# Attention scores in quarters of the array, with both sequences in one stacking transfer

## What is computed

```python
x = x + _L0_xattn_ref(_layernorm(x), ctx_1024, ctx_1024, ...)
#   scores = einsum('bhqd,bhkd->bhqk', q, k) / sqrt(8); softmax; @ v; @ Wo.T + bo
x = x + _L0_ffn_ref(_layernorm(x), ...)
#   out_branch: top 32 of softmax(gate_out) times (x @ weight)
#   in_branch:  (x times top 32 of softmax(gate_in)) @ weight
```

## Time and profile before

| | us |
|---|---|
| median of 3 runs (558.95 to 564.75) | 564.16 |
| the profiled execution | 563.33 |
| its span, first to last instruction | 560.8 |
| attention stage, to the first top-k work | about 311 |
| top-k stage and its end | about 250 |

### The profile page before, as it was taken

How to read it: one execution, slowest core, us unless ns; L and a number is a source line. 1 busy time by engine, 2 the same in 40 slices (tenths; PEclk the granted TensorE clock), 3 DMA queues, 4 the chain that set the end, 5 groups by cost and what they waited for, 6 DMA issues and landing times.

```text
span 560.8 us, 15570 instructions
## 1 busy us (share of the span) xinstructions
PE 405.9 (72%) x5186; PEld 316.1 (56%) x5186; DVE 440.5 (79%) x2165; ACT 375.1 (67%) x1060; POOL 330.2 (59%) x402
## 2 busy tenths in 40 slices
PE   3467988999998999988992766666666666666432
PEld 1135766777777777777860545545555555445331
DVE  7745666777877777776541799999999999999990
ACT  2425676877788777766655967777677666676652
POOL 6466676887677777562112046666666666666666
PEclk9857999999999999999795555555555555555555
DMA  4888786888887887675000000000000000000000
GB/s 135 177 206 207 193 199 151 194 185 185 192 195 191 206 187 185 161 168 123 4 4 1 0 2 19 19 20 20 19 20 19 20 20 19 20 20 19 19 20 19
DMA packets 138680, 52.78 MB, mean 94 GB/s; under 512 B 105115, under 2 KB 130908, under 8 KB 137052
## 3 DMA queue, kind: packets, MB, share of 16 engines
q1 hardware_dynamic: 136424, 51.27, 37.8%
q10 hardware_dynamic: 2176, 0.52, 0.4%
HBM read 34.47 MB, written 16.78 MB: 91 GB/s over the span
## 4 chain that ended last, share of the span: by engine, by line
DVE 41%; SPq 33%; DMA 9%; PE 7%; issue 5%; POOL 2%; ACT 2%; POOLq 0%; ACTq 0%; DVEq 0%
SPq L273 30%; DVE kst L868 22%; DVE top_next L859 12%; DMA k_scratch<-k_parts 6%; DVE top_first L859 4%; DMA qst<-q_scratch 3%; SPq L258 3%; PE ps_pv L329 1%; PE ps_col L314 1%; POOL kst L963 1%; ACT x2n L550 1%; PE ps_mix L534 1%; PE ps_row L358 1%; PE ps_row L503 1%; SPq L220 1%
## 5 line engine op out<-in xcount | busy, mean ns | idle before, releaser
L738 DVE TENSOR_REDUCE m<-ps_row 128x8 f32<-128x512 f32 x128 | 82.4, 686 | 54.5 <-PE ps_row L358 54.2
L868 DVE MATCH_REPLACE8 kst<-top_next,kst 128x128 f32<-128x128 f32 x384 | 101.2, 282 | 0.0
L545 ACT ACTIVATE pT<-ps_col 128x512 f32<-128x512 f32 x128 | 68.7, 589 | 37.1 <-PE ps_col L314 37.1
L859 DVE MAX8 top_next<-kst 128x8 f32<-128x128 f32 x384 | 78.2, 282 | 0.0
L329 PE MATMUL ps_pv<-vx,pT 128*64 128x18 f32 x2048 | 72.5, 213 | 0.0
L329 PEld LDWEIGHTS ps_pv<-vx,pT 128*64 128x64 f32 x2048 | 66.1, 139 | 6.3 <-issue 4.2
L519 PE MATMUL ps_proj<-wf_sb,x2T 128*128 128x128 f32 x128 | 33.2, 441 | 45.8 <-ACT x2T L682 45.8
L519 PEld LDWEIGHTS ps_proj<-wf_sb,x2T 128*128 128x128 f32 x128 | 28.5, 328 | 52.2 <-ACT x2T L682 52.2
L550 ACT ACTIVATE x2n<-xr,nm,rs 128x128 f32<-128x128 f32 x128 | 52.6, 493 | 4.2 <-POOL nm L888 4.2
L959 POOL TENSOR_SCALAR neg_max<-top_first 128x4 f32<-128x4 f32 x32 | 7.1, 222 | 74.8 <-DVE top_first L859 74.8
L358 PE MATMUL ps_row<-kst,qst 96*64 96x128 bf16 x1024 | 42.3, 226 | 12.1 <-DMA qst<-q_scratch 12.0
(11 more groups left out here) (103 smaller groups left out, 1092.7 us busy)
## 6 DMA issues: line engine op xcount, KB each, us to landing
k_scratch<-k_parts SPq DMA_DIRECT2D x32, 192.0 KB, 3.1
q_scratch<-q_parts SPq DMA_DIRECT2D x32, 192.0 KB, 3.0
kst<-k_scratch SPq DMA_DIRECT2D x32, 192.0 KB
qst<-q_scratch SPq DMA_DIRECT2D x32, 192.0 KB
xr<-in_x_dram SPq DMA_DIRECT2D x16, 256.0 KB, 4.3
cT<-in_ctxT_dram SPq DMA_DIRECT2D x16, 256.0 KB, 3.7
kst<-k_scratch SPq DMA_DIRECT2D x32, 128.0 KB
qst<-q_scratch SPq DMA_DIRECT2D x32, 128.0 KB
```

Source lines behind the costliest of these rows:

```text
L545: act.activation(pT[:, b % PT_RING, :, :], ps_col[b % 2][:, :, :], ACT.Exp, scale=SCALE).then_inc(act_exp, 1)
L738: dve.tensor_reduce(m32[:, b // 4, :, 4 * j:4 * j + 4].rearrange("q a h -> q h a"), ps_row[b % 2][:, :, :, :], AX.X, ALU.max).then_inc(dve ...
L859: ins = dve.max(top[:, n, :], src)
L868: ins = dve.match_replace(picked[s][:, p, cols], top[:, n, :], src, PICKED)
```

## The change

- `kst` and `qst` of a slot are two halves of one tensor `stacks[s]`. Half a's 48 stacked rows now lie in partitions 64 a to 64 a + 63, and `kst` has no block of zeros any more; its row is 8 KB in one run. The products are three neighbouring pairs of parts (`RUNS`), each with both halves in one transfer: partitions run, run + 4, ... to 127, for keys and for queries, 6 transfers in all. The fourth of every four partitions is zero but for four rows (`MAX_ROWS`: 3, 35, 67, 99) with minus ones on the key side and maxima on the query side, reset by one more transfer from `fixed_rows`.
- Scores are computed by half: 64 by 64 matmuls over 64 rows, four positions in the array by turns, twice as many as before.
- The maxima transfer goes from ACT to SP (`maxima`), and SP's and PE's order changes with it.
- DVE splits the first group's keys, computes part of the first and of the last group's norm, the gates' constants, and the last group's end; POOL's query split waits for `dve_m`. At the start ACT loads the key and query weights.

```diff
-RUNS = (3, 2, 1)
+MID, HIGH, LOW = 0, 1, 2
+RUNS = ((MID, MID), (HIGH, MID), (MID, HIGH))
+MAX_ROWS = slice(3, 128, 32)
...
-STACK = 16 * 2 * len(RUNS)
+STACK = 16 * (2 * len(RUNS) + 1)
...
+        scratch = [nc.dram_tensor(f"scratch{s}", (2, 2 * PARTS, 128, HALF), BF16).ap() for s in range(2)]
...
-            def stack(g, scratch, done, moved, to_keys):
+            def two_parts(g, first):
+
+                return scratch[g % 2][:, first:first + 2].rearrange("a n (i h) t -> a (n i) (h t)", h=HEADS)
+
+            def stack(g):
                 s, d = g % 2, slot(g)
-                wait(sp, done[s], WRITES * (g // 2 + 1))
-                for a in range(2):
-                    for n in RUNS:
...
+                wait(sp, k_out[s], WRITES * (g // 2 + 1))
+                wait(sp, q_out[s], WRITES * (g // 2 + 1))
+
+                wait(sp, pe_col, 8 * (g - STACKS + 1))
+
+                sp.dma_start(qst[d][MAX_ROWS, :, :].rearrange("r h t -> r (h t)"), fixed_rows[4:8]).then_inc(moved[d], 16)
+                for run, (q_first, k_first) in enumerate(RUNS):
+
+                    rows = slice(run, 128, 4)
+                    sp.dma_start(kst[d][rows, :, :].rearrange("r h t -> r (h t)"),
+                                 two_parts(g, PARTS + k_first)).then_inc(moved[d], 16)
+                    sp.dma_start(qst[d][rows, :, :].rearrange("r h t -> r (h t)"),
+                                 two_parts(g, q_first)).then_inc(moved[d], 16)
+
+            def maxima(g, hp):
+                wait(sp, act_mT, 2 * g + hp + 1)
+                wait(sp, moved[slot(g)], STACK * uses(g))
+                sp.dma_start(qst[slot(g)][MAX_ROWS, :, hp * 128:(hp + 1) * 128], mT[:, hp, :]).then_inc(m_moved[hp][slot(g)], 16)
...
+                if there(t - 1):
+                    maxima(t - 1, 1)
                 if there(t + 1):
-
-                    wait(sp, act_mT, 2 * t)
-                    wait(sp, pe_col, 8 * (t - 1))
-                    stack(t + 1, k_scratch, k_out, k_moved, True)
-                    stack(t + 1, q_scratch, q_out, q_moved, False)
+                    stack(t + 1)
+                if there(t):
+                    maxima(t, 0)
                 if there(t + 2):
...
+                for hh in range(HEADS // 2):
+                    h = j * (HEADS // 2) + hh
+                    for pp, a in ((0, 0), (1, 1), (1, 0), (0, 1)):
+                        rows = slice(a * 64, a * 64 + 64)
+                        cols = slice((2 * hp + pp) * SEQ, (2 * hp + pp + 1) * SEQ)
+                        mm = pe.matmul(ps_row[a][pp * SEQ:(pp + 1) * SEQ, hh, :], qst[s][rows, h, cols], kst[s][rows, h, cols],
+                                       start=True, stop=True)
...
                 if d:
                     key_side(t - 1, 0, 0)
+                if c:
+                    query_side(t, 0, 0)
                 if e:
                     out_proj(t - 2, 0)
...
                 if d:
                     turn_max(t - 1, 1)
                 if e:
                     values(t - 2, 1, 1)
+
+                if d:
+                    key_side(t - 1, 0, 1)
                 if c:
-                    query_side(t, 0)
-                    query_side(t, 1)
-
-                if d:
-                    key_side(t - 1, 0, 1)
+                    query_side(t, 0, 1)
```

More of the change, by code:

```diff
@@ L236, in _, with write_parts @@
             sp.dma_start(gates[2 * GATES:2 * GATES + 1, :], ones_row).then_inc(rest_in, 16)
-            for s in range(STACKS):
-                if s == 1:
-                    sp.wait_ge(gp_zero, 1)
-                else:
-                    sp.wait_ge(dve_zero, s // 2 + 1)
-                if s == 2:
-                    load_x(2)
-                sp.dma_start(kst[s][MROWS:KROWS, :, :, :, :].rearrange("r h p a m -> r (h p a m)"), minus_rows).then_inc(rows_in, 16)
-            def write_parts(g, parts, scratch, done, moved):
+            def write_parts(g, parts, first, done):
                 s = g % 2
                 if parts is k_parts:
-                    wait(sp, gp_split, 4 * g + 4)
+                    wait(sp, dve_ksplit, 4)
+                    wait(sp, gp_split, 4 * g)
                 else:
@@ L465, in _ @@
                     values_in(t)
-                if c:
                     turn_max(t, 0)
@@ L478, in _ @@
                     key_side(t - 1, 1, 1)
+                if c:
+                    query_side(t, 1, 1)
                 if n:
@@ L644, in _ @@
                     wait(act, gp_rs2, 4 * (t - 2) + 4)
+                    wait(act, dve_nm2, 1 if t - 2 == GROUPS - 1 else 0)
                     wait(act, pe_x2T, t - 3)
@@ L707, in _ @@
                     ins.then_inc(a2_yin, 1)
+                if t == GROUPS:
+                    wait(act, p2_yin, GROUPS - 1)
+                    for half, bank in enumerate((ps_pv, ps_turn)):
+                        cols = slice(half * 256, half * 256 + 256)
+                        wait(act, p2_xsT, GROUPS + half)
+                        act.activation(xsT[:, cols], bank[:, cols], ACT.Copy).then_inc(a2_xsT, 1)
                 if t >= 1 and there(t + 1):
@@ L850, in _ @@
                     top = top_first[s] if rnd == 0 else top_next
+                    by_gate = g == GROUPS - 1 and rnd == 3
+                    sets = (range(1, 8, 2), range(0, 8, 2)) if by_gate else (range(0, 4), range(4, 8))
                     for half in range(2):
@@ L854, in _ @@
                         else:
-                            wait(dve, d2_rep, 8 * g + 2 * rnd - 1 + half)
-                        for n in range(4 * half, 4 * half + 4):
+                            wait(dve, d2_rep, 8 * g + 2 * rnd - 1 + (1 if by_gate else half))
+                        for n in sets[half]:
                             p, cols = chain(n)
```

425 lines of the change are left out of this document (237 added, 188 removed).

## The result

The changed kernel takes 926.69 us (median of 4 runs, 925.67 to 926.96) where the kernel before takes 563.23 (558.95 to 564.75): the ratio is 1.650, interval 1.642 to 1.658. It is slower by 65%, and 5 us under the predicted 932.

What follows compares the result with a forecast made beforehand. Bound: stacks on two DMA engines in series with a PE, ACT, SP chain. Issue at 56.7, 14 rounds of 39.3 (550.2), last stack 31.6, rest 290.9: span 929.4, plus 2.5, predicted 932 us; range 855 to 1040.

Steps and rivals of the forecast that it cites:

- Number of engines: New stacking transfers: with 2 sequences outermost in the source, two DMA engines carry each, 16 rows apiece, and 14 idle.
- Cost of a stack, 31.6 us: One group's stacking: 96 rows of 8 KB per engine at 0.316 us make 30.3 us, plus 1.3 start and landing.
- Chain, 7.7 us: Between stacks: PE 5.5 us, ACT's copies 1.0, two SP issues 1.2, in series behind each landing; round 39.3 us.
- rival (b): All 16 engines, quarters don't overlap: 30 ns floor per score matmul, 128 more cost 3.8 us; 592 us, chance 0.05.
- Writes hidden in the chain: Next group's scratch writes, landing about 4.5 us, are covered by the 7.7; without that cover the longer counts, not the sum.
- The sign that missed: Profile after the change: the chain of waits would name DMA `stacks`<-`scratch`, with PE, ACT and SP pieces of about 8 us.
- The other signs: 2 closing packets per stacking transfer, DMA share near 0.2, score matmuls every 39 us, clock falling in gaps, top-k stage unchanged.
- The rest, 290.9 us: From the last stack's landing to the end: 295.9 us before, less about 5 from the last group's chain and gates' constants.
- the start: First group: stack issue at 20 us, and stack 0 landing at 51.6 us.
- Rival (a): All 16 engines carry the stack and quarters overlap, so PE bounds at 13.9 us a round; 533 us, chance 0.09.
- the −2 and −5: Terms of the 533 us sum with 16 engines: 2 us and 5 us saved outside the rounds.
- the −24: Term of the 533 us sum with 16 engines: 16 rounds each 1.5 us shorter, PE bounding at 13.9 us at most.

Runs made afterwards that it cites:

- Experiment 1: Changed kernel, but each stacking transfer's source is 32 rows at one stride (wrong parts, time only) in place of 2 x 16: 548.20 us, ratio 0.978.
- experiment 2: Changed kernel, but each stacking transfer's source is 4 pieces of 8 rows (wrong parts, time only) in place of 2 of 16: 695.96 us, ratio 1.237.
- experiment 3: Changed kernel with 4 stacking transfers a group in place of 6, the third run of rows left out: 766.86 us, ratio 1.363.
- experiment 4: Changed kernel, but PE turns and ACT copies the second half's maxima before the next stack's first score block: 881.46 us, ratio 1.573.
- experiment 5: Changed kernel, but ACT issues the two maxima transfers right behind its copies, and SP issues none: 884.00 us, ratio 1.576.
- experiment 7: Changed kernel, but each of six stacking transfers takes one half's queries and keys together, 16 rows outermost on both sides: 561.02 us, ratio 1.001.
- experiment 6: Changed kernel with each half moved on its own, 12 stacking transfers of 16 rows a group in place of 6: 574.08 us, ratio 1.025.
- experiment 8: Changed kernel with halves moved apart (12 transfers) and the maxima turned and copied before the next stack's first score block: 567.07 us, ratio 1.012.
- experiment 9: Changed kernel with one half's queries and keys in one transfer, and maxima turned and copied before the next stack's first score block: 575.29 us.
- experiment 10: Changed kernel with halves moved apart (12 transfers) and the two maxima transfers issued by ACT: 557.98 us, ratio 0.997.
- experiment 11: Changed kernel with one half's queries and keys in one transfer, and the two maxima transfers issued by ACT: 567.44 us, ratio 1.013.

## Why the prediction was right, step by step

- **Number of engines: right.** The step rested on the destination's side and left the source's side unproven. Experiments 1 and 2 prove it there, and experiment 3 counts the two closing packets.
- **Cost of a stack, 31.6 us: 33.1.** The row rate held (0.316 taken, 0.3125 measured between experiment 3 and the changed kernel). Start and landing were taken as 1.3 us from an output transfer (2.0 − 0.6 is 1.4); experiment 3's pair gives 2.9.
- **Chain, 7.7 us: 6.2.** From the landing at 320.84 the clock was low as expected, but PE needed 4.2 us to the end of `turn_max` (325.04) and not 5.5; ACT took 0.7 for 1.0, SP 1.3 for 1.2. The pieces of the chain of waits of the changed kernel:

```profile
320.88 0.64 PE ps_col L322 x27
321.52 0.43 PE ps_row L371 x26
321.95 1.15 PE ps_mix L354 x4
323.10 1.71 PE ps_proj L393 x2
324.81 0.23 PE ps_turn L384
```

  All run at the lower clock (granted 0.50 from 320.9 to 325); what I had over for it was too much, since the two score blocks, 1.9 us in my sum at full clock, are only 1.1 us of it (see rival (b)). That the round came out at 39.3 is luck in part: the two errors, +1.5 for the stack and −1.5 for the chain, cancel, and 39.31 is the round shown. Its mean over all groups is less: the first query block starts at 53.13 and the last group's at 630.91, which is 577.8 / 15 = 38.5 us.
- **Writes hidden in the chain: right, with little room.** Experiments 4 and 5 took the first chain away, and the writes then allowed the next issue 2.8 and 2.5 us after the landing. That is where "the longer of the two" begins to count. What I had not seen is that SP itself is held by them (11.5 and 8.1 us); it was idle time here and on the path in experiment 5.
- **The sign that missed.** The chain of waits was to name `stacks`<-`scratch`; it names `stacks`<-`mT`, 42%, with `stacks`<-`scratch` at 3%. The prediction had the reason: the maxima are issued behind the six transfers and wait for the same moment. The other signs came: two closing packets, a DMA share of 0.21, a round of 39.3, a clock of 0.50 in the gaps, and a top-k stage as it was.
- **The rest, 290.9 us: 293.1** (924.0 − 630.9), where 295.9 stood before. In the sum, the start came 1.5 us later than thought (53.1 for 51.6), the mean rounds shorter, the rest 2.2 longer: 924.0 for 929.4.
- **Rival (a), 16 engines and quarters that overlap, 533 us.** Its gain was put too high. Experiment 1 shows this case nearly pure, at 548. Its first query block starts at 32.99 and the last group's at 254.84, so 14.79 us a round where I gave 13.9; the start, 34.6 to 33.0, and the rest, 295.9 to 290.1, are the −2 and −5 of the sum (−1.6 and −5.8). What failed is the −24: it is −8.6 (15 × 0.57). The stretches show why:

The kernel before, 80 to 240 us (columns as in the earlier trace rows):

```profile
80.00:240.00 160.00, 149.52 (x3011) 118.92 (x3008) 118.30 (x365) 124.62 (x275) 116.88 (x169) 1.00 0.79 185
```

Experiment 1, the same stretch:

```profile
80.00:240.00 160.00, 149.14 (x4600) 116.59 (x4599) 130.61 (x386) 130.61 (x289) 125.52 (x179) 1.00 0.63 196
```

PE is busy for 149 of 160 us in both. SP, which led the chain before, thus held the round by no more than 0.6 us beyond what PE and its waits for DVE and ACT allow; taking SP away gives back that, not the gaps of PE. (Two small sums of this rival are off as well: 15.7 less the gaps is 14.0, and 4 + 1.3 + 7 is 12.3.)

- **Rival (b), a floor of 30 ns for each matmul: wrong.** The changed kernel at full clock, PE's timeline:

```profile
331.78 0.45 PE L322 MATMUL ps_col<-stacks 64*64 64x64 bf16 x32
332.05 0.60 PE L371 MATMUL ps_row<-stacks 64*64 64x64 bf16 x32
332.59 0.71 PE L354 MATMUL ps_mix<-wo_sb,attnT 128*128 128x128 f32 x4
```

32 matmuls of a quarter take 0.27 us to the next block's start (331.78 to 332.05), 8.4 ns each, and 0.54 us in the next block; 16 took 0.48 us before. So the 30 ns of before were no floor for a matmul as such. The Trainium skill ("TensorE: Matmul & The Clock Gate", section "Back-to-back issue gap") has a floor near 25 ns. Between matmuls on different quarters the trace shows 8.4 ns at full clock, so that figure does not price them; the measurement decides.

## What to carry to other kernels

Before two transfers are merged into one, read the outermost count of both sides: a source of 2 pieces is carried by 2 engines, however many rows lie under each, and the packets of the queue's row tell it (one closing packet for each engine and transfer). A rearrangement that halves the issues thus cost 23.6 us a group here (378 us over 16, experiment 1). And where the next long transfer's issue waits, through other engines, for a short one that stands behind a long one in the same queue, every landing becomes part of a serial chain: that was 43 us with two engines and 16 us with sixteen. So price the order as well as the bytes.

## What the runs showed of the hardware that I had not expected

- The number of engines follows the outermost count of the source as well as that of the destination: with 32 outermost in the destination, 2, 4 and 32 in the source gave 192, 384 and 1536 closing packets over 96 transfers (q1: 39,416, 39,608, 40,760).
- Score matmuls on different quarters start 8 to 17 ns apart at full clock (0.27 and 0.54 us for 32).
- A short transfer from ACT's queue landed ahead of a stack that SP had issued before it, 9.5 us after its issue; from SP's own queue it took 24.3 us (experiment 5).
- SP is held when it issues transfers while two engines have much queued: two issues of `k_parts` took 11.55 us in the changed kernel, and 0.91 us with 16 engines on the stack:

```profile
134.47 0.91 SPq L249 DMA_DIRECT2D scratch<-k_parts  x2
```

(experiment 1, SP's queue.) This hold-up of SP cost nothing in the changed kernel and lay on the chain in experiment 5.
- 16 rows with two pieces of 8 KB under each took the engines 13 us longer over the kernel than 32 rows with one (experiments 7 and 6; the profiles of 8 to 11 agree); the cause was not tried.
